# Attention layer with two causal attentions: longer runs of score slots, three key banks, projections from split operands

## The reference

```
q, k = split(x @ W_attn + b)         # 16 heads of 16
v    = heads of x
y    = causal_attn(q, k, v)          # softmax(q k^T / 4) v
e    = v[1:] - y[:-1]
k2   = x[:-1] @ W_k2 + b_k2
y2   = causal_attn(q[1:], k2, e)     # shifted down by one row
x1   = layernorm(x + y W_proj + y2 W_proj + 2 b_proj)
```

## Time and profile before

| | |
|---|---|
| runs, median (range) | 2620.78 us (2616.14 to 2626.06) |
| profiled execution | 2615.51 us |
| its span, mean granted clock | 2613.8 us, 0.986 |
| PE, DVE, ACT, POOL busy | 95%, 81%, 67%, 53% |
| row maxima, L820, in PSUM operations | 1689.6 us |
| exponential, L498 | x2560, mean 598 ns |
| bias of a piece, L516 | x192, mean 687 ns |
| split of a piece, L442 and L444 | x192, mean 611 and 1279 ns |
| negated rows, request to landing | 2.1 us |

### The profile page before, as it was taken

The page is one execution under the profiler, slowest core; times in us unless marked ns, Lnnn a source line. Parts: engine busy times, 40 slices in busy tenths (PEclk is TensorE's granted clock), DMA queues, the critical chain, the costliest instruction groups (busy, mean ns, idle before and its releaser), DMA issues.

```text
span 2613.8 us, 64356 instructions
## 1 busy us (share of the span) xinstructions
PE 2477.4 (95%) x19286; PEld 1215.6 (47%) x19286; DVE 2123.0 (81%) x9392; ACT 1763.8 (67%) x3388; POOL 1397.3 (53%) x2214
## 2 busy tenths in 40 slices
PE   3999999999999999999999999999999999999997
PEld 1444444444444444444444444444444444444444
DVE  2788888888888888888888888888888888888755
ACT  0377777677777766777777677777776777777652
POOL 2355555555555555555555555555555555555432
PEclk8699999999999999999999999999999999999999
DMA  5455555565555546555555565555556555554211
GB/s 96 87 105 87 93 94 101 98 116 103 104 92 95 101 91 111 108 106 95 93 96 97 103 116 103 101 91 94 103 90 115 104 107 95 92 100 86 67 53 52
DMA packets 187779, 251.18 MB, mean 96 GB/s; under 512 B 26769, under 2 KB 103193, under 8 KB 187417
## 3 DMA queue, kind: packets, MB, share of 16 engines
q1 hardware_dynamic: 187440, 247.07, 51.7%
HBM read 74.60 MB, written 16.78 MB: 35 GB/s over the span
## 4 chain that ended last, share of the span: by engine, by line
PE 79%; issue 7%; DVE 6%; ACT 5%; POOL 3%; SPq 1%; DMA 1%; ACTq 0%; POOLq 0%; DVEq 0%
PE score_t L627 22%; PE out_t L588 21%; PE misc L692 14%; PE score L638 9%; PE misc L727 5%; PE turn L670 5%; DVE junk L820 3%; ACT prob L498 2%; PE score L775 1%; ACT y_t L530 1%; PE misc L714 1%; POOL prob L422 1%; DVE resid L871 1%; PE score L791 1%; DVE max_cols L820 1%
## 5 line engine op out<-in xcount | busy, mean ns | idle before, releaser
L820 DVE CUSTOM_DVE_ANT_0 junk<-score,mask_rows 128x384 bf16<-128x384 f32 (+3 forms) x3584 | 1689.6, 514 | 378.5 <-PE score L638 374.8
L498 ACT ACTIVATE prob<-score_t 128x512 f32<-128x512 f32 x2560 | 1403.6, 598 | 614.4 <-PE score_t L627 609.6
L422 POOL TENSOR_SCALAR_AFFINE_SELECT prob<-prob 128x512 f32<-128x512 f32 (+1 forms) x1280 | 726.5, 569 | 1046.2 <-ACT prob L498 1046.1
L627 PE MATMUL score_t<-stack_q,stack_k 50*128 50x128 f32 (+5 forms) x4096 | 1052.7, 364 | 45.0 <-ACT prob L498 34.0
L638 PE MATMUL score<-stack_k,stack_q 48*128 48x512 f32 (+3 forms) x4096 | 1040.1, 352 | 9.8 <-DMA stack_q<-part_l 7.7
L627 PEld LDWEIGHTS score_t<-stack_q,stack_k 50*128 50x128 f32 (+1 forms) x4096 | 600.7, 185 | 778.2 <-ACT prob L498 673.3
L588 PE MATMUL out_t<-prob,value 128*32 128x512 f32 (+3 forms) x8192 | 711.3, 442 | 0.0
L638 PEld LDWEIGHTS score<-stack_k,stack_q 48*128 48x128 f32 x4096 | 607.8, 188 | 27.2 <-DVE max_cols L820 16.0
L692 PE MATMUL misc<-x_t,wq 128*128 128x512 f32 x512 | 285.4, 641 | 60.8 <-DMA bias<-L_attn_b_proj 31.3
L820 DVE DVE_READ_ACCUMULATOR2_ANT max_cols<- 128x1 f32 x4096 | 337.2, 82 | 0.0
L588 PEld LDWEIGHTS out_t<-prob,value 128*32 128x32 f32 x8192 | 187.5, 108 | 312.3 <-issue 215.1
(11 more groups left out here) (83 smaller groups left out, 1233.7 us busy)
## 6 DMA issues: line engine op xcount, KB each, us to landing
stack_k<-part_h SPq DMA_DIRECT2D x512, 128.0 KB, 4.2
stack_k<-part_l SPq DMA_DIRECT2D x256, 128.0 KB, 4.5
stack_q<-part_h SPq DMA_DIRECT2D x256, 128.0 KB, 4.1
x_t<-x_turned SPq DMA_DIRECT2D x32, 512.0 KB, 9.5
x_in<-L_attn_x SPq DMA_DIRECT2D x32, 512.0 KB, 14.1
stack_q<-part_l SPq DMA_DIRECT2D x128, 128.0 KB, 5.1
resid<-L_attn_x SPq DMA_DIRECT2D x32, 512.0 KB, 6.2
layer_out<-resid SPq DMA_DIRECT2D x31, 512.0 KB, 5.4
```

The costliest lines, as they stand in the source:

```text
L422: e.affine_select(out=view, in_=view, compare_op=ALU.is_ge, fill=0.0, base=-unit_parts(unit)[1], pattern=[[0, runs], [0, cut], [1, P]], ch ...
L498: e.activation(prob[pair % RING][:, slot % 2 * 512:slot % 2 * 512 + 512], score_t[time % KEY_DEPTH][:, :], ACT.Exp, scale=1.0 / np.sqrt(HE ...
L627: done = e.matmul(score_t[now % KEY_DEPTH][:, col:col + n], keys[rows, pair, kb * P:(kb + 1) * P], stack_q[b % 2][rows, pair, kb * P:token ...
L820: e.tensor_tensor_reduce(junk[count % JUNK][:, 0:n], score[number % MAX_DEPTH][:, col:col + n], mask, 1.0, -3e38, ALU.add, ALU.max, max_co ...
```

## The change

- `RUNS`: TensorE issues slots 0 to 2 together, then 3 to 5 at slot 3, then 6 to 9 at slot 6. `KEY_DEPTH` is 3.
- There is no bank `turn`. The heads are transposed into `out_t`, after ScalarE has copied it; the maxima into `misc`, at slot 2.
- Weighted values: block 0 at slot 9, after the normalisation of the unit before; blocks 1, 3 and 2 together at slot 2 of the next unit. Values are 17 columns wide instead of 32. `out_t` is zeroed once.
- `x` and the projection weights are split in float32r parts: the weights once, on VectorE; x per batch, on GpSimd, in place 6. Each half of a piece is three float32r matmuls. One tile for x in full instead of two; its load is at slot 8 of place 0, for the next batch.
- y is transposed at slot 2, its projection in halves at slots 5 and 9 of places 3 and 6; residual added at slot 0 of places 4 and 7; statistics in place 7; normalisation in place 0 of the next batch, the output's load and store later to match.

Left out of the diff below: semaphore declarations, the renamed tiles and first loads.

```diff
@@ -49,7 +49,9 @@
...
-RING, KEY_DEPTH, MAX_DEPTH, JUNK = 6, 2, 3, 2
+RING, KEY_DEPTH, MAX_DEPTH, JUNK = 6, 3, 3, 2
...
+RUNS = {0: (0, 1, 2), 3: (3, 4, 5), 6: (6, 7, 8, 9)}
@@ -102,15 +104,18 @@
...
-        value1 = sb("value1", [P, blocks, HEADS, 32])
-        value2 = sb("value2", [P, blocks, HEADS, 32])
+        wq_full = nc.alloc_sbuf_tensor_at("wq_full", [P, halves, 2 * halves, P], F32, offset=prob_at + 4 * pairs * tokens)
+        wk2_full = nc.alloc_sbuf_tensor_at("wk2_full", [P, halves, halves, P], F32, offset=prob_at + 5 * pairs * tokens)
+        value1 = sb("value1", [P, blocks, HEADS, HEAD_DIM + 1])
+        value2 = sb("value2", [P, blocks, HEADS, HEAD_DIM + 1])
...
-        x_t = [sb(f"x_t{i}", [P, halves, tokens]) for i in range(2)]
+        x_full = sb("x_full", [P, halves, tokens])
+        x_t = [sb(f"x_t_{part}", [P, halves, tokens], F32R) for part in "hl"]
@@ -133,17 +138,17 @@
@@ -320,12 +324,12 @@
...
-                if (place, slot) == (0, 8) and 2 <= b < batches:
-                    e.wait_ge(s_piece, N_PIECES * (b - 1))
-                    e.dma_start(x_t[b % 2][:, :, :], x_turned[b].rearrange("(h p) t -> p h t", p=P)).then_inc(s_xt[b % 2], 16)
+                if (place, slot) == (0, 8) and 1 <= b < batches:
+                    e.wait_ge(s_xsplit, 2 * halves * b)
+                    e.dma_start(x_full[:, :, :], x_turned[b].rearrange("(h p) t -> p h t", p=P)).then_inc(s_xt, 16)
...
-                if (place, slot) == (1, 8) and 0 <= b < batches:
+                if (place, slot) == (2, 2) and 0 <= b < batches:
@@ -360,8 +364,8 @@
...
-                b = ahead - 1
-                if (place, slot) == (6, 0) and 1 <= b < batches:
+                b = ahead - 2
+                if (place, slot) == (1, 0) and 1 <= b < batches:
@@ -422,7 +426,7 @@
...
-                if (place, slot) == (2, 5) and 0 <= ahead - 1 < batches:
+                if (place, slot) == (3, 2) and 0 <= ahead - 1 < batches:
@@ -442,6 +446,19 @@
...
+                for c in range(halves):
+                    b = ahead + 2
+                    if (place, slot) == (6, (4, 7)[c]) and 0 <= b < batches:
+                        if c == 0:
+                            e.wait_ge(s_xt, 16 * (b + 1))
+                            if b:
+                                e.wait_ge(s_piece, N_PIECES * b)
+                        e.tensor_copy(x_t[HIGH][:, c, :], x_full[:, c, :]).then_inc(s_xsplit, 1)
+                        e.wait_ge(s_xsplit, 2 * (halves * b + c) + 1)
+                        e.tensor_tensor(x_t[LOW][:, c, :], x_full[:, c, :], x_t[HIGH][:, c, :].bitcast(F32),
+                                        ALU.subtract).then_inc(s_xsplit, 1)
@@ -465,11 +482,11 @@
...
-                if (place, slot) == (4, 7) and 0 <= b < batches:
+                if (place, slot) == (7, 6) and 0 <= b < batches:
...
-                if (place, slot) == (4, 9) and 0 <= b < batches:
+                if (place, slot) == (7, 8) and 0 <= b < batches:
@@ -498,14 +515,6 @@
...
-                for a, b in ((0, ahead + 1), (1, ahead)):
-                    if (place, slot) == ((7, 1), (3, 1))[a] and 0 <= b < batches:
-                        m = 2 * b + a
-                        e.wait_ge(s_neg_pe, m + 1)
-                        if m:
-                            e.wait_ge(s_maxrow[1 - a], 16 * MAX_PARTS * SIDES * (b + a))
-                        e.activation(neg_h[:, :], turn[0:64, 0:P], ACT.Copy, scale=-1.0).then_inc(s_negh, 1)
@@ -515,14 +524,22 @@
...
-                if slot == 3 and 0 <= unit - 1 < end:
+                if slot == 2 and 0 <= unit - 1 < end:
...
+                for a, b in ((0, ahead + 1), (1, ahead)):
+                    if (place, slot) == ((7, 2), (3, 2))[a] and 0 <= b < batches:
+                        m = 2 * b + a
+                        e.wait_ge(s_neg_pe, m + 1)
+                        if m:
+                            e.wait_ge(s_maxrow[1 - a], 16 * MAX_PARTS * SIDES * (b + a))
+                        e.activation(neg_h[:, :], misc[0:64, 0:P], ACT.Copy, scale=-1.0).then_inc(s_negh, 1)
...
-                    if (place, slot) == ((1, 4), (2, 4))[hf] and 0 <= ahead - 1 < batches:
+                    if (place, slot) == ((1, 2), (2, 2))[hf] and 0 <= ahead - 1 < batches:
@@ -530,10 +547,11 @@
...
-                if (place, slot) == (4, 8) and 0 <= b < batches:
+                if (place, slot) == (7, 7) and 0 <= b < batches:
...
-                if place == 5 and slot in (1, 3, 5, 7) and 0 <= b < batches:
-                    apply_norm(e, b, slot // 2, x1_routed if b == 0 else resid, resid)
+                b = ahead - 2
+                if place == 0 and slot in (2, 4, 6, 8) and 0 <= b < batches:
+                    apply_norm(e, b, slot // 2 - 1, x1_routed if b == 0 else resid, resid)
@@ -585,7 +604,7 @@
...
-                    done = e.matmul(out_t[32 * h:32 * h + 32, first:first + count], value[:, kb, GROUP * g + h, :],
+                    done = e.matmul(out_t[32 * h:32 * h + HEAD_DIM + 1, first:first + count], value[:, kb, GROUP * g + h, :],
@@ -595,8 +614,8 @@
...
-                for now in (time, time + 1) if slot % 2 == 0 else ():
-                    at = now % SLOTS
+                for at in RUNS.get(slot, ()):
+                    now = SLOTS * unit + at
@@ -641,33 +660,16 @@
...
-                if slot == 7 and 0 <= unit < end:
-                    b, a, g = unit_parts(unit)
-                    if a:
-                        e.wait_ge(s_value2, GROUPS * b + g + 1)
-                    elif g == 0:
-                        e.wait_ge(s_value1, b + 1)
-                    if unit:
-                        e.wait_ge(s_heads, unit)
-                    weigh(unit, 0, 0, tokens, start=True)
-                if 0 <= unit - 1 < end:
-                    if slot == 1:
-                        weigh(unit - 1, 1, P, 3 * P)
-                        weigh(unit - 1, 3, 3 * P, P)
-                    if slot == 3:
-                        weigh(unit - 1, 2, 2 * P, 2 * P, stop=True)
+                if slot == 2 and 0 <= unit - 1 < end:
+                    weigh(unit - 1, 1, P, 3 * P)
+                    weigh(unit - 1, 3, 3 * P, P)
+                    weigh(unit - 1, 2, 2 * P, 2 * P, stop=True)
...
-                    if unit >= 2:
-                        e.wait_ge(s_normal, unit - 1)
-                    if place == 7 and ahead + 1 < batches:
-                        e.wait_ge(s_negl, 2 * (ahead + 1) + 1)
-                    if place == 3:
-                        e.wait_ge(s_negl, 2 * ahead + 2)
...
-                        done = e.transpose(turn[:, t * P:(t + 1) * P], heads_t[:, t * P:(t + 1) * P], ident[:, :])
+                        done = e.transpose(out_t[:, t * P:(t + 1) * P], heads_t[:, t * P:(t + 1) * P], ident[:, :])
@@ -678,8 +680,9 @@
...
+                                e.wait_ge(s_wsplit, 4)
...
-                                e.wait_ge(s_xt[b % 2], 16 * (b // 2 + 1))
+                                e.wait_ge(s_xsplit, 2 * halves * (b + 1))
@@ -687,24 +690,32 @@
...
-                                e.wait_ge(s_attended, 2 * ahead)
-                        w = wk2[:, c, hf, :] if kind == "k2" else wq[:, c, hf + (0 if kind == "q" else halves), :]
-                        done = e.matmul(misc[:, :], w, x_t[b % 2][:, c, :], start=(c == 0), stop=(c == halves - 1))
+                                e.wait_ge(s_attended, 2 * ahead - 1)
+                            if place == 7 and ahead + 1 >= 0:
+                                e.wait_ge(s_negl, 2 * ahead + 3)
+                        for i, (pw, px) in enumerate(zip(PARTS_K, PARTS_Q)):
+                            w = wk2[pw][:, c, hf, :] if kind == "k2" else wq[pw][:, c, hf + (0 if kind == "q" else halves), :]
+                            done = e.matmul(misc[:, :], w, x_t[px][:, c, :], start=(c == 0 and i == 0),
+                                            stop=(c == halves - 1 and i == TERMS - 1))
...
-                    if (place, slot) == ((7, 1), (3, 1))[a] and 0 <= b < batches:
+                    if (place, slot) == ((7, 2), (3, 2))[a] and 0 <= b < batches:
...
-                        if unit >= 2:
-                            e.wait_ge(s_normal, unit - 1)
-                        e.transpose(turn[0:64, 0:P], max_cols[b % 2][:, a, :, :, :].rearrange("p s h q -> p (s h q)"),
+                        e.wait_ge(s_full, min(N_PIECES * (b + 1) + (4 if a else 0), N_PIECES * batches))
+                        if ahead >= 1:
+                            if a:
+                                e.wait_ge(s_yt, halves * ahead)
+                            else:
+                                e.wait_ge(s_attended, 2 * ahead)
+                        e.transpose(misc[0:64, 0:P], max_cols[b % 2][:, a, :, :, :].rearrange("p s h q -> p (s h q)"),
...
-                        if (place, slot) == ((1, 3), (2, 3))[hf]:
+                        if (place, slot) == ((1, 2), (2, 2))[hf]:
@@ -715,19 +726,31 @@
...
```

(38 more changed lines are left out.)

23 lines of the change are left out of this document (11 added, 12 removed).

## The result

The changed kernel takes 2638.8 us (median of 4 runs, 2634.3 to 2641.2); the kernel before took 2618.5 beside it (4 runs, 2615.1 to 2626.1). The ratio is 1.0072, with a 95% interval of 1.0044 to 1.0099: slower by 0.7%, where 2604 and faster was forecast. The time lies inside the range 2490 to 2670, the sign is wrong. The profiled execution took 2637.9 us (span 2636.2, mean granted clock 0.973), against 2615.5 (2613.8, 0.986).

What follows compares the result with a forecast made beforehand. TensorE was taken to set the pace, with VectorE's maxima withholding most of the saving: 0.53 us a batch over 31.4 batches, -17, all else 0, so 2599 profiled and 2620.8 - 17 = 2604 median; range 2490 to 2670.

Steps and rivals of the forecast that it cites:

- rival C: Place 7's waits halve TensorE's clock in each batch, doubling about 1.9 us: 76.8 a batch, 2664; chance 0.13.
- the sum: Whole kernel: batch saving and ends added up, giving 2599 for the profiled execution and 2604 for the median.
- All else is taken as 0, bounds -10 and +10: Outside steady batches: weight splitting, shorter starting projections and the queued last normalisation together change nothing, within -10 to +10.
- the -17 for the batches: Steady part: 0.53 us saved per batch over 31.4 batches, 17 us less.
- The schedule: Eight units of a steady batch timed slot by slot: 74.88 us against 75.41; chance 0.60.
- The slot-9 wait: In each unit slot 9 needs slot 6's bank, held by VectorE's maxima until 6.40; TensorE waits 1.1 us.
- the signs of being wrong: TensorE over 95% busy, slot 9 held by ScalarE, batch under 72 or over 77 us, clock below 1.00 inside batches.
- taken as 0.87: Projection half of three float32r matmuls: 0.87 us instead of 1.05, saving 0.18.
- rival B: Projections: float32r parts cost no less with 128 rows; 2638 (chance 0.10) or 2719 (0.05), 0.15 in all.
- the working's 0.39 and 1.05: TensorE in the kernel before: turn ahead of a projection 0.39 us, projection group 1.05 us.
- The third key bank takes the keys off this wait: At slot 9: slot 6's exponential ends near 5.8, so the keys' bank doesn't add to the wait on VectorE.
- rival A: Slot 9's wait doesn't come; TensorE's own sum of 64.0 us a batch holds, 2263; chance 0.09.

Runs made afterwards that it cites:

- e5_tail: Changed kernel with the last batch's second output projection and normalisation moved ahead of the end of the experts' work; 2634.2 us, ratio 1.0064.
- e2_runs: Changed kernel without the operand split (float32 projections again), keeping runs, banks, moved steps and 17 columns; 2691.4 us, ratio 1.0280.
- e7_fill: Changed kernel with overwritten 512-column matmuls ahead of the first projection half, 5 in place 7 and 3 in place 5; 2628.4 us, ratio 1.0042.
- e1_parts: Kernel before with only the float32r operand split and the values of 17 columns; 2573.7 us, ratio 0.9834.
- e9_short: Changed kernel with each row maximum taken over only the first 64 columns of its score block; 2395.4 us, ratio 0.9145.
- e3_late9: Changed kernel with slot 9's scores behind the second projection half instead of before it; 2456.5 us, ratio 0.9388.
- e10_tailfill: Changed kernel with 5 and 3 filler matmuls at places 7 and 5, plus six ahead of slot 6 in places without a projection; 2622.9 us, ratio 1.0016.
- e11_pairs: Changed kernel with 5 and 3 filler matmuls at places 7 and 5, and scores in pairs of slots in the last five units; 2630.5 us, ratio 1.0042.
- e8_best: Changed kernel with slot 9 late, statistics over places 6 and 7, unread last-batch projection halves, last normalisation earlier; 2429.0 us, ratio 0.9281.

## Why the prediction was wrong

The range was wide enough to reach the clock's rival C, so that the time lies in it says nothing for the sum, which gave 2599 for the profiled execution and 2604 for the median.

**The step that failed** is "All else is taken as 0, bounds -10 and +10". It is +22.7 by the table of stretches (all rows but the thirty batches: 1.82 + 3.80 + 6.90 + 6.67 - 0.45 + 3.93). Only the start and the queued normalisation (+3.9, and `e5_tail` gives it back) had been named. Of the start's +1.8 the split of the weights can be at most 0.7: `e2_runs`, which splits nothing, needs 88.13 us for it. The first batch's +3.8 goes with a half-rate stretch of 6.8 us; `e5_tail`, with one of 3.4 us instead, takes 74.85, which is +1.8. The units without projections had been counted as steady ones: the first of them, a place 7, has TensorE idle for 2.5 us in four waits for VectorE, where the steady place 7 has 1.8 in three, and the clock falls (0.83 in 40.65 us; with it up they take 36.4). How the 6.67 of the stretch behind them divide is not shown. Both could have been looked for, since the earlier trace rows show the clock falling behind a wait near the end of the kernel.

**The second step that failed** is the -17 for the batches. The schedule itself was right: 74.88 a batch forecast, 75.04 measured. From slot 0 to slot 0, places 0 to 7 measured 8.97, 9.34, 9.35, 9.35, 8.86, 9.25, 9.13 and 10.79, forecast 8.93, 9.31, 9.31, 9.36, 8.84, 9.08, 9.13 and 10.92. (These are the eight units from 1230.99 us on.) The slot-9 wait is there in each unit, VectorE waits ahead of slot 0 in each and ahead of slot 3 in five of the eight, place 7 is the longest. With the clock up (`e7_fill`) the thirty batches take 2251.3 us against 2265.5 before, -14.2; half rate gave +13.9 of it back. A clock below 1.00 inside the batches stood among the signs of being wrong, and it came. Rival C named the right place and mechanism, and the wrong amount: it doubled 1.9 us in each batch (2664, chance 0.13); it came in seven of thirty batches only, 1.5 to 2.7 us a stretch, in the mean 0.46 a batch. It is not a case of its own beside the schedule but a cost that belongs to the schedule's waits. With it and the ends at their true size the same sum gives 2615.5 - 14.2 + 13.9 + 22.7 = 2637.9, the profiled time.

**Sizes.** A projection half takes 0.88 (0.86 to 0.90), taken as 0.87; rival B is out. The turn ahead of it takes 0.50 in the kernel before and the half behind it 0.95; the working's 0.39 and 1.05 have nearly the same sum. In the old grouping the split, with the 17 columns, collects 1.39 of 12 x 0.16 = 1.9 a batch (`e1_parts`), in the new one 1.10 (76.14 to 75.04), since half of the halves stand ahead of a wait; the working had said that. The 17 columns, taken as nothing, are worth some 0.3 a batch. The Trainium skill ("TensorE: Matmul & The Clock Gate", section Back-to-back issue gap) gives about 131 ns for N=512; three such matmuls at 0.86 to 0.90 the group don't agree, as no row before did.

**A second holder behind the first.** "The third key bank takes the keys off this wait" holds in the changed kernel: slot 6's exponential ends 1.24 us after slot 6's start (1254.51 to 1255.75), as forecast (4.58 to 5.8), and the maxima come 0.4 later. But it holds only as long as VectorE is the slower one. By `e9_short` ScalarE alone holds slot 9 for 0.49 a unit, and the working's own numbers had it: 5.8 is later than the 5.50 at which slot 9 could start. For this reason rival A's 2263 was not to be had: it gave TensorE's sum, and 68.33 a batch is what is left without VectorE.

**What was missed.** The comparison of the two orders: a wait costs what is queued behind it, and the projection half behind slot 9 was in the schedule as a term, not asked about. `e3_late9` shows that this one place in the order was worth 5.4 us a batch.

## What to carry to other kernels

Cost the stretches that are not steady (start, the units after the last of a kind of work, the last chain) with the same working as the steady one; here they held +22.7 us where the whole difference is +22.4. Where a new order makes TensorE wait for a bank, ask what independent work is queued behind that wait and put it ahead, before anything is saved in the matmuls themselves. A wait of TensorE has a second price, the clock of what comes after it: look at the granted clock by stretches, not at its mean.

## What the runs showed of the hardware

- Waits of TensorE inside otherwise full batches bring its clock to half. In the changed kernel six of eight stretches began in or just after place 7's waits (in the case shown, waits of 0.31 us ahead of slot 8 and 1.28 us ahead of slot 9; the granted clock was 0.50 for 6.8 us from within the second). Matmuls whose results nobody reads, put into the waits, left none in the thirty batches in two kernels (`e7_fill`, `e10_tailfill`) and one in a third (`e11_pairs`), against 5 to 9 in three executions without them. Where TensorE waits less, the thirty batches have none either: in the batches whose rows were taken it is idle for 1.0 us in `e3_late9`, 0.9 in `e8_best` and 2.1 in `e9_short`, against 7.0 in the changed kernel and 2.2 in the kernel before. The Trainium skill ("TensorE: Matmul & The Clock Gate", section A second HAM failure mode: psum-queue depth-cycling) tells of a kernel in which short idle times between matmul groups, from cycling through PSUM banks, made the clock swing; the trace agrees.
- It is not the busy share alone that orders it: from 300 to 2400 us TensorE was busy for 1903 us with 7 stretches, in `e2_runs` for 1924 us with 16, in `e7_fill` for 1941 us with none. What it wants is open.
- A float32r matmul with 128 rows and 512 columns takes no longer than one with 48 to 52 rows: halves of three take 0.86 to 0.90 in `e1_parts` and in the changed kernel, where a group of three 512-column slots takes 0.90.
